# Recurrence stage: second norm and feed-forward one slot later, residual behind the second scan, mixing products in two banks

## What is computed

```python
xa = _ln(x, ln1_w, ln1_b)
sx = concatenate([state[:, 1:2] - xa[:, :1], xa[:, :-1] - xa[:, 1:]], axis=1)
xxx = tanh((xa + sx * maa_x) @ maa_w1).reshape(b, l, 5, 32)
xxx = einsum('blfd,fde->blfe', xxx, maa_w2)
xm = xa[:, :, None] + sx[:, :, None] * (maa_stack + xxx)
xk, xw, xv, xr, xg = (xm[:, :, j] for j in range(5))
w = exp(-exp(time_decay + tanh(xw @ td_w1) @ td_w2))
r, k, v, g = xr @ Wr.T, xk @ Wk.T, xv @ Wv.T, silu(xg @ Wg.T)
# per token and head: a = k outer v; out = r (u a + s); s = a + w s
og = ((out - m) / sqrt(var + 1e-5)) * gn_w + gn_b      # mean and variance over the 8 of a head
x1 = x + og * g @ Wo.T
xc = _ln(x1, ln2_w, ln2_b)
sx2 = concatenate([state[:, 0:1] - xc[:, :1], xc[:, :-1] - xc[:, 1:]], axis=1)
rr = sigmoid((xc + sx2 * ffn_maa_r) @ Wfr.T)
kk = square(relu((xc + sx2 * ffn_maa_k) @ Wfk.T))
return x1 + rr * (kk @ Wfv.T)
```

## Time and profile before

| what | us |
|---|---|
| median of three runs (2136.38 to 2137.86) | 2136.49 |
| the profiled execution | 2138.01 |
| its span | 2136.3 |
| stage of the recurrence, from DVE's first `shift_a` to the end | 1776.5 to 2136.3 |
| busy over the span: PE, DVE, ACT, POOL | 1944.2, 1261.8, 1085.0, 516.4 |

### The profile page before, as it was taken

The page is one execution under the profiler, slowest core; times in us unless marked ns, Lnnn a source line. Parts: engine busy times, 40 slices in busy tenths (PEclk is TensorE's granted clock), DMA queues, the critical chain, the costliest instruction groups (busy, mean ns, idle before and its releaser), DMA issues. The chain is left out here.

```text
span 2136.3 us, 40585 instructions
## 1 busy us (share of the span) xinstructions
PE 1944.2 (91%) x15496; PEld 1692.5 (79%) x15496; DVE 1261.8 (59%) x2546; ACT 1085.0 (51%) x2920; POOL 516.4 (24%) x346
## 2 busy tenths in 40 slices
PE   6999996999999999999899999999988986898974
PEld 4677764997999999999699999999978984566653
DVE  6888886235645555555465555555552364888883
ACT  3787877545443344443453344334446543566653
POOL 3555453544200000000240000000005514324220
PEclk9999998999999999999999999999998997899986
DMA  5000001300000000002200000000020000000000
GB/s 188 2 2 2 2 2 42 117 1 6 6 6 5 0 5 5 5 5 90 74 6 1 5 5 5 5 0 5 29 89 1 1 1 1 1 11 6 6 11 10
DMA packets 29534, 40.72 MB, mean 19 GB/s; under 512 B 1923, under 2 KB 21477, under 8 KB 29157
## 3 DMA queue, kind: packets, MB, share of 16 engines
q1 hardware_dynamic: 29412, 39.06, 5.4%
HBM read 32.76 MB, written 2.10 MB: 16 GB/s over the span
## 5 line engine op out<-in xcount | busy, mean ns | idle before, releaser
L761 DVE TENSOR_TENSOR w_head_lo<-banks,w_head_hi 128x512 fp32r<-128x512 f32 x128 | 88.1, 691 | 249.5 <-ACT w_head_hi L673 241.9
L692 ACT ACTIVATE arena<-banks 128x512 f32<-128x512 f32 x128 | 74.9, 597 | 295.1 <-PE banks L551 291.0
L727 DVE TENSOR_TENSOR arena<-banks,cols 128x512 f32<-128x512 f32 x128 | 88.6, 692 | 227.0 <-PE banks L118 226.8
L470 POOL TENSOR_TENSOR w_hT_lo<-arena,w_hT_hi 128x512 fp32r<-128x512 f32 x16 | 20.9, 1306 | 821.0 <-ACT w_hT_hi L647 821.0
L685 ACT ACTIVATE arena<-banks,arena 128x129 f32<-128x129 f32 x512 | 181.3, 376 | 39.5 <-DVE arena L741 39.5
L964 POOL TENSOR_TENSOR arena<-arena 128x1024 f32<-128x1024 f32 x64 | 150.4, 2373 | 162.2 <-DVE arena L1250 162.2
L673 ACT ACTIVATE w_head_hi<-banks 128x512 fp32r<-128x512 f32 x128 | 76.5, 598 | 196.1 <-PE banks L561 196.0
L1168 ACT ACTIVATE arena<-arena 128x128 f32<-128x128 f32 x512 | 163.5, 397 | 1.8 <-DVE arena L1259 1.6
L116 PE MATMUL banks<-w_wo_lo,w_head_hi 128*128 128x256 f32 x512 | 148.6, 290 | 1.3 <-DVE w_head_lo L761 1.3
L116 PE MATMUL banks<-w_hT_lo,w_hi 128*128 128x256 f32 x512 | 146.6, 286 | 0.0
L116 PE MATMUL banks<-w_kv_lo,w_hi 128*128 128x256 f32 x512 | 145.2, 284 | 0.2
(11 more groups left out here) (299 smaller groups left out, 5702.9 us busy)
## 6 DMA issues: line engine op xcount, KB each, us to landing
arena<-in_L_xattn_wq SPq DMA_DIRECT2D x8, 512.0 KB, 4.9
arena<-in_L_xattn_wk SPq DMA_DIRECT2D x8, 512.0 KB, 6.0
arena<-in_L_xattn_wv SPq DMA_DIRECT2D x8, 512.0 KB, 6.9
arena<-in_L_xattn_wo SPq DMA_DIRECT2D x8, 512.0 KB, 9.5
arena<-ctx_t SPq DMA_DIRECT2D x16, 256.0 KB, 2.5
x<-in_x SPq DMA_DIRECT2D x4, 512.0 KB, 6.6
ctx_t<-in_ctx_t SPq DMA_DIRECT2D x1, 2048.0 KB, 11.7
arena<-in_L_xattn_w SPq DMA_DIRECT2D x2, 1024.0 KB, 12.8
```

The source lines that it names most:

```text
L692: act.activation(probT[:, b, :, :], bank[5 + b][:, :].rearrange("p (h q) -> p h q", h=HG), ACT.Copy).then_inc(probT_ok, 1)
L727: dve.tensor_tensor(qT[:, h:h + 2, :], bank[use % 2][:, :].rearrange("p (h t) -> p h t", h=2), core.col(bias, g * HG + h, 2)[:, :, None].t ...
L761: dve.tensor_tensor(head_lo[:, two, :], bank[5 + half][:, :].rearrange("p (h t) -> p h t", h=2), head_hi[:, two, :], ALU.subtract).then_in ...
```

## The change

Six things move, all within `recurrence`.

- `MIX` names the bank of each of the five mixing products: X, Y, Z, X, Y before, now Y, X, Y, X, Y. Each of the last three waits until the product before the last has been read. The wait for the group variance (bank Z) passes from the third product to `low_rate`. Products 0 and 1 of pair p+2 are issued at the end of slot p, between `sum_heads(p, 3)` and `centre(p)`; product 1 waits for `make_bonus(p+1)` (bank X).
- `normalise2`, `copy_xc`, `square_relu`, `sigmoid_rr`, `c_transpose`, `project_kk`, `project_rr`, `project_ff`, `row_shift`, `shift_c`, `gate_ff` and `finish` run for pair p−2 (flag `d`) and not p−1, so the slots go to 9. `row_rstd(p-1)` stays, at the slot's end. In slot 8 alone the steps of pair 6 are placed earlier.
- `project_out` moves behind `project_r`; `residual` behind `scan(p, 2)`.
- `multiply_rk` and `times_gate` go from POOL to DVE.
- `a_transpose` stands directly behind `c_transpose`, both in bank Y, and waits for `copy_xc(p-2)`; `normalise(p+2)` moves ahead of `tanh_g` on ACT.
- `spread_v(p+1, 0)` moves ahead of `project_ff`, and `a_low` and `bonus_sums` ahead of `sum_heads(p, 3)`; DVE's `shift_a` ahead of unit 3.

The core of the diff (the waits of the slots' ends and repeated parts left out):

```diff
-        MIX = [X, Y, Z, X, Y]
+        MIX = [Y, X, Y, X, Y]
...
-            for p in range(-1, NP + 1):
+            for p in range(-1, NP + 2):
...
@@ gpsimd @@
+                if exists(p + 1):
+                    add_xa(p + 1, range(0, F))
+                if exists(p - 2):
+                    finish(p - 2)
@@ tensor @@
-                wait(pe, read["xc"], a - 2)
+                wait(pe, read["xc"], a - 3)
...
-            def a_mix(a):
+            def a_mix(a, fs):
                 pe.wait_ge(read["low"], a + 1)
-                for f in range(F):
-                    if f == 0:
+                for f in fs:
+                    if f == 1:
                         wait(pe, read["c"], a)
-                    elif f == 2:
-                        wait(pe, read["var"], a - 1)
-                    elif f > 2:
-                        pe.wait_ge(f_read, a * F + (f - 2))
+                    elif f > 1:
+                        pe.wait_ge(f_read, a * F + (f - 1))
...
             def low_rate(a):
                 pe.wait_ge(mix_ok, a * F + FW + 1)
-                pe.wait_ge(f_read, a * F + 3)
+                wait(pe, read["var"], a - 1)
...
             def project_out(c):
                 pe.wait_ge(z_ok, c + 1)
                 pe.wait_ge(read["td"], min(c + 3, NP))
+                if c == NP - 1:
+                    pe.wait_ge(read["kk"], c)
...
             def project_kk(c):
                 pe.wait_ge(xk_ok, c * (2 * KC) + KC)
-                pe.wait_ge(read["out"], c + 1)
+                if c == NP - 2:
+                    pe.wait_ge(read["var"], NP)
+                else:
+                    pe.wait_ge(read["out"], min(c + 2, NP))
@@ scalar, slot(p) @@
                 if c:
                     square_centred(p - 1)
-                if a:
-                    tanh_low(p + 1)
+                if d:
+                    normalise2(p - 2)
                 if c:
                     group_rstd(p - 1)
+                if d and p == NP:
+                    copy_xc(p - 2)
...
+                if d:
+                    square_relu(p - 2)
+                    sigmoid_rr(p - 2)
                 if c:
-                    square_relu(p - 1)
-                    sigmoid_rr(p - 1)
+                    row_rstd(p - 1)
                 if exists(p + 2):
-                    copy_xa(p + 2)
+                    tanh_low(p + 2)
```

More of the change, by code:

```diff
@@ L2111, in slot @@
                     project_v(p + 1)
-                if c:
-                    project_out(p - 1)
+                if p == NP:
+                    c_transpose(p - 2)
+                    project_kk(p - 2)
                 if u:
@@ L2298, in slot @@
                     copy_r(p + 1)
-                if c:
-                    normalise2(p - 1)
+                if exists(p + 2):
+                    normalise(p + 2)
                 if a:
                     tanh_g(p + 1)
-                if c:
-                    copy_xc(p - 1)
+                if d and p != NP:
+                    copy_xc(p - 2)
                 if a:
@@ L2442, in slot @@
                     mix(p + 1)
+                if d and p == NP:
+                    shift_c(p - 2)
                 if c:
@@ L2445, in slot @@
                 if u:
-                    unit(p, 1)
+                    weigh_keys(p, 1)
+                    scan(p, 1)
+                if c:
+                    times_gate(p - 1)
+                if u:
+                    times_r(p, 1)
+                    weigh_keys(p, 2)
+                    scan(p, 2)
                 if c:
```

113 lines of the change are left out of this document (56 added, 57 removed).

## The result

The changed kernel takes 2143.79 us (median of seven executions, 2142.36 to 2146.74), the kernel before beside it 2136.38: a ratio of 1.0035, interval 1.0026 to 1.0044. It is slower by about a third of a per cent, where the prediction said 0.7% faster. The profiled execution has a span of 2142.0 us against 2136.3.

What follows compares the result with a forecast made beforehand. A chain hopping between engines bounds the steady slot: 7.9 + 15.4 + 10.3 + 0.8 = 34.4 us, with clock toll x = 35.1. Total change 6x − 225.7 = −15.1, giving 2121.4 us from 2136.5; range 2110 to 2131.

Steps and rivals of the forecast that it cites:

- slots 2 to 6: Five steady slots, each `make_bonus` to `make_bonus`: 35.1 us each, against 186.85 us for all five before.
- slot 1: Slot after the second `make_bonus`: a steady slot less 2.9 us, having neither `shift_c` nor `gate_ff`; 38.8 us before.
- fill and slot 0: Stage up to the second `make_bonus`: −0.2 us, bounds −2 and +2, with `bonus_sums` now behind `a_low`.
- drain: From `make_bonus(7)` to the end, 70.6 us before: +3 us, with the last 18.0 us from `row_shift(7)` unchanged.
- the clock's toll: Steady slots' loss to PE's lowered clock: 1.2 us before, half of it, 0.6, expected after.
- each take 0.57, so DVE is not starved: Mixing products 2 to 4 on PE: each waits for one DVE read of 0.84 us and takes 0.57.
- a cover of 0.15 us: `residual` behind the second scan: `project_out` ready at 20.25, DVE arriving at 20.4, so the 1.00 us wait goes.
- DVE's floor: DVE's busy time per steady slot: 32.8 − 2.0 (`times_r` stretches) + 1.4 (two products from POOL) = 32.2 us.
- rival 2: Steady slots: the clock's toll stays whole or grows, x = 36.4 to 37.2, 2129 to 2134 us; 0.20 with the fourth.
- rival 3: Every slot: PE at 1.2 GHz for some 40%, granted clock 0.80, x = 38.6, 2142 us; chance 0.05.
- signs of being wrong: Granted clock in slots outside 0.92 to 1.00, fifth POOL add meeting the scan, fill or drain moving over 3 us.
- the fourth: `centre` waits for the next slot's `make_bonus`, group norm 1.5 us later, x = 36.5; chance 0.20 together with rival 2.

Runs made afterwards that it cites:

- The kernel with a single row group: Kernel before, with all five mixing products reading operands from rows 0 to 31: 2139.27 against 2137.18 us, ratio 1.0010.
- the two banks alone: Kernel before, with only the mixing part changed (banks Y and X alternating, old order): 2143.26 against 2137.73 us, ratio 1.0020.
- the halved products: Changed kernel, with mixing products 2 to 4 of pairs 1 to 7 computing only half their features: 2133.66 against 2136.66 us for the kernel before.
- the third product moved ahead: Changed kernel, with mixing product 2 between `centre` and `variance`, products 3 and 4 in one piece behind: 2140.82 us against 2137.37 for the kernel before.
- The filler: Changed kernel, with one unread product per pair on PE between `centre` and `variance`: 2142.69 us against 2137.73 for the kernel before, ratio 1.0026.
- `row_shift` late: Changed kernel, with `row_shift(p-2)` behind `weigh_keys(p,0)` and `make_bonus(p)` on DVE: 2142.12 us against 2137.18 for the kernel before, ratio 1.0026.
- the three edits: Changed kernel, with `bonus_sums` ahead of `a_low`, `row_shift` behind `make_bonus`, and pair 7's `project_out` and `row_rstd` earlier in slot 8: 2132.91 us, ratio 0.9982 to kernel before.
- all of it: the three edits, plus mixing product 2 ahead of `variance` and `group_rstd` ahead of `normalise2` on ACT: 2119.33 against 2137.73 us for the kernel before.

## Why the prediction was wrong

The span was to change by −15.1 us and changed by +5.7. The 20.8 us between them are, by the terms of the prediction: slots 2 to 6, 9.0 (184.5 against 5 × 35.1); slot 1, 4.6 (36.8 against 32.2); fill and slot 0, 5.7 (+5.5 against −0.2); drain, 1.6 (+4.6 against +3). The steps that failed are the price of a single mixing product, the queue on PE where the pipeline fills, which the sum left at nothing, and the clock's toll.

**The steady slot at full clock: 35.60, not 34.4.** The forecast's chain, taken apart at the same points:
- from `make_bonus` to `unit_variance` 8.5 was forecast, and 9.57 measured (1994.10 to 2003.67). Product 1 takes 1.12 and not 0.57 before `centre` can start, so that the group norm on ACT ends at 2003.43, 9.3 us behind `make_bonus` (row below). `mix` ends later still: products 2 to 4 stand behind `centre`, the wait for the square and `variance` on PE, and with two banks each goes alone. So the path goes through the mixing products, and the group norm would be next: it ends 0.24 us ahead of `unit_variance`. This is the step that failed first: "each take 0.57, so DVE is not starved". The kernel with a single row group and the two banks alone show the price, and the halved products that it was on the path.
- from `unit_variance` to `project_kk` 15.4 was forecast, 16.0 measured, with the 0.88 before `residual`. I had given that a cover of 0.15 us and said that any slower product would show; the late mix ate it up. With the third product moved ahead 0.14 of it was left.
- from `project_kk` to the next `make_bonus` 9.7, measured 10.0. Here I had missed that POOL's `finish` (1991.77, 1.26 us) runs just when `row_shift` comes. The two SBUF operands of an instruction of 128 × 2 elements are enough: 0.13 us of work took 0.77. The forecast had the wait before it (0.3, measured 0.59), not the clash. Its price is small all the same: `bonus_sums`, the other thing that `make_bonus` needs, ended only 0.4 us ahead of it. This is the earlier trace rows's exclusion once more, in an instruction too small to be suspected.
- the hand-overs, 0.8 in the sum, lie inside these measured stretches: 9.57 + 16.02 + 10.01 = 35.60.

```profile
2002.80 0.63 ACT L2234 ACTIVATE arena<-arena 128x512 f32<-128x512 f32 x1
```

DVE's floor was sized well: 32.2 forecast, 32.36 busy in slot 5 with the stretch of 0.64 in it. The four waits (0.96, 0.43, 0.88, 0.59) come to 2.86, and they make up nearly all that the slot is longer.

**The clock's toll: 1.3, not 0.7.** Four of the five slots were granted 0.95 and took 37.2. I expected the toll to halve with the 2 us wait gone. It stayed whole, as rival 2 had it (1.2 before). The low stretch moved from `project_kk` to `project_k` and `project_v`, and either costs the slot its full price: before, `project_kk` took 3.5 us and not 1.99 in slots 2 and 3, which took 37.6 and not 36.14; after, the two took 5.41 and not 3.72, in slots of 37.2 and not 35.60. What brings the clock down stays open. The filler speaks against the wait before `variance` as the one cause. In four kernels shorter slots went along with more of them at full clock (half of the products, `row_shift` late, the three edits, all of it), but the third product alone had two slots at 0.91, and the kernel before had both 1.00 and 0.87 without any difference in its order.

**Slot 1 and what comes ahead of it.** The prediction took −0.2 ± 2 for fill and slot 0, and for slot 1 a steady slot without `shift_c` and `gate_ff`. Both terms left out that PE's new order is one queue: `bonus_sums`, which `make_bonus` needs, stands behind `a_low`, and this behind `spread_v` of the next pair, which waits for DVE. In a steady slot that fits; where the pipeline fills, it doesn't (PE idle 4.67, DVE idle 3.66, 1.97 and 2.58). I named the new place of `bonus_sums` in one clause and didn't price it. Turning the two round showed it for what comes ahead of slot 1: the stage up to `make_bonus(1)` was then 0.2 us shorter than in the kernel before, which is the −0.2 of the forecast. For slot 1 it showed little: 36.1 and not 36.8, so that 3.9 of its 4.6 us stay. 1.2 of them are the steady slot's own, and the rest stands with the waits in `mix` and the granted clock of 0.86 and was not taken apart; slot 1 came down to 34.2 with the third product moved ahead, and to 32.7 with all five edits.

**Drain: +4.6, not +3.** `row_shift(7)` came 56.1 us behind `make_bonus(7)`, forecast 54.7 and up to 1.9 more; and the last 18.0 us, which I took as unchanged, took 19.1, because `project_rr` and `project_ff` of the last pair ran longer at the low clock, 4.75 and not 3.66 us (2131.72 after, 2127.08 before):

```profile
2127.08 3.66 PE L1991 MATMUL banks<-arena 128*128 128x256 f32 x16
```

```profile
2131.72 4.75 PE L1973 MATMUL banks<-arena 128*128 128x256 f32 x16
```

**What was right**: the fate of POOL's work and of `times_r`, the 1.1 us wait in the transpositions (1.35), the count of DVE's floor, and the clock of the steady slots (0.95 to 1.00): rival 3's 0.80 did not come. Of the signs of being wrong three did: fill by 5.5 us, drain by 4.6, and slot 1 with a granted clock of 0.86. Of the rivals the second and the fourth (x of 36.4 to 37.2) held the steady slot, 36.9, though by other waits than theirs; with x = 36.9 the formula gives 6 × 36.9 − 225.7 = −4.3, and the rest of the way to +5.7 is the 10 us by which fill, slot 1 and drain came out above their terms. My range let the ends vary by 2.

## What to carry to other kernels

A duration per product read from a group of several is a price for that group: before reusing it for one product, see whether the group ran side by side, and on which rows of the array. When work is moved within an in-order queue, price the first and the last rounds with their own waits, not as a steady slot less some work; here they decided the sign. And a shorter critical chain shows its full worth only when the next two or three waits that take its place are moved as well: one by one the edits that were tried alone gave at most 0.35 us in a slot at full clock, and all of them, with ACT's order changed too, 1.65.

## What the runs showed of the hardware

- Two matrix products of 32 rows on different row groups of PE take 1.14 us, one alone or each on the same group 1.12.
- `row_shift` (128 × 2, two operands in SBUF) takes 0.13 to 0.16 us alone and 0.77 beside a POOL addition that had begun 0.5 us earlier; it ends with POOL's. The Trainium skill, page "SBUF — State Buffer", section "Summary: rules for kernel authors", says that of a DVE instruction with two inputs in SBUF and a POOL one that reads SBUF the later is blocked until the first is done; the trace agrees, down to this size.
- The same order of instructions gave slots with a granted clock of 1.00 and of 0.95, 1.7 us apart, in one execution, and an otherwise idle 0.4 us filled with a product changed neither.
